# Row statistics moved to the attention stage, a split second quantiser and six unread products in the FFN stage

## The reference, cut to what matters

```
h   = h + attn(layernorm(h))
x   = layernorm(h)                                     # 192 wide
g   = gelu(quant(rmsnorm(x) * g1) @ ternary(w1).T)     # 768 wide
out = h + quant(rmsnorm(g) * g2) @ ternary(w2).T
quant(x) = round(x * 127 / max(|x|)) / (127 / max(|x|))   # per row
```

## Time and profile before

| | us |
|---|---|
| median of three runs | 1888.55 (1887.67 to 1893.47) |
| profiled execution, its own time | 1889.4 |
| its span in the trace | 1887.7 |
| attention stage with filling | about 128 to 1360 |
| FFN stage | about 1360 to 1887.7 |

### The profile page before, as it was taken

How to read it: one execution, slowest core, us unless ns; L and a number is a source line. 1 busy time by engine, 2 the same in 40 slices (tenths; PEclk the granted TensorE clock), 3 DMA queues, 4 the chain that set the end, 5 groups by cost and what they waited for, 6 DMA issues and landing times.

```text
span 1887.7 us, 50796 instructions
## 1 busy us (share of the span) xinstructions
PE 1579.8 (84%) x16574; PEld 1297.6 (69%) x16574; DVE 1364.8 (72%) x3151; ACT 1283.7 (68%) x1958; POOL 1089.7 (58%) x1503
## 2 busy tenths in 40 slices
PE   0539999999999999999999999999466666666666
PEld 0427788888888888888888888887345555555555
DVE  3636676767767676767676767676389999999996
ACT  1226666766767676767676666665288888888887
POOL 5035555555555555555555555554177777777775
PEclk9869999999999999999999999999666666666665
DMA  8674666665657565756565666660000000000000
GB/s 102 141 127 59 95 87 96 86 99 83 103 79 104 83 99 83 99 88 94 89 94 91 91 93 88 94 87 25 17 16 21 21 21 22 22 22 22 22 22 26
DMA packets 159967, 132.96 MB, mean 70 GB/s; under 512 B 32558, under 2 KB 151040, under 8 KB 159808
## 3 DMA queue, kind: packets, MB, share of 16 engines
q1 hardware_dynamic: 159168, 131.00, 44.4%
q0 software_dynamic: 768, 1.57, 0.5%
HBM read 118.32 MB, written 11.91 MB: 69 GB/s over the span
## 4 chain that ended last, share of the span: by engine, by line
PE 66%; DVE 15%; issue 7%; SPq 3%; ACT 3%; DMA 3%; POOL 1%; DVEq 1%; ACTq 0%; POOLq 0%
PE ps L1092 20%; PE ps L1176 8%; PE ps L1259 7%; PE ps L1250 7%; PE ps L1206 4%; DVE ff_st L860 4%; PE ps L1238 3%; PE ps L1232 3%; PE ps L1211 3%; PE ps L1336 2%; PE ps L1355 2%; DVE xpix L841 2%; PE ps L1167 2%; DVE xpix L853 1%; PE ps L1157 1%
## 5 line engine op out<-in xcount | busy, mean ns | idle before, releaser
L1092 PE MATMUL ps<-w_eff,pix 118*112 118x193 f32 (+1 forms) x2048 | 408.4, 337 | 25.0 <-ACT pix L909 24.3
L927 ACT ACTIVATE probs<-ps,isw 116x688 f32<-116x688 f32 x384 | 299.2, 831 | 171.6 <-PE ps L1238 171.6
L527 POOL TENSOR_TENSOR xpix<-probs,g_b 112x192 f32<-112x192 f32 (+1 forms) x512 | 296.5, 609 | 109.1 <-ACT probs L1044 99.7
L741 DVE TENSOR_REDUCE nmax<-ps 116x12 bf16<-116x1344 f32 (+2 forms) x192 | 299.6, 1560 | 80.2 <-PE ps L1211 77.7
L452 POOL TENSOR_TENSOR xsq<-xsq 118x784 f32<-118x784 f32 (+2 forms) x192 | 221.8, 1155 | 218.5 <-ACT xsq L920 208.4
L1092 PEld LDWEIGHTS ps<-w_eff,pix 118*112 118x112 f32 (+1 forms) x2048 | 309.8, 167 | 52.4 <-issue 18.9
L472 POOL TENSOR_SCALAR_AFFINE_SELECT probs<-probs 116x464 f32<-116x464 f32 x384 | 268.2, 717 | 46.5 <-ACT probs L927 31.0
L909 ACT ACTIVATE pix<-xpix 118x896 f32<-118x896 f32 (+1 forms) x128 | 198.4, 1552 | 104.9 <-DMA xpix<-in_x 56.0
L457 POOL TENSOR_TENSOR front_st<-front_st,expo 128x2 f32<-128x2 f32 x64 | 45.0, 703 | 235.2 <-DVE front_st L693 221.2
L1336 PE MATMUL ps<-w1t,xpix 96*112 96x384 f16 (+1 forms) x512 | 160.7, 488 | 14.6 <-ACT xpix L1035 13.3
L685 DVE TENSOR_SCALAR front_st<-ps 112x1 f32<-112x1 f32 (+1 forms) x128 | 18.3, 151 | 213.8 <-PE ps L1157 202.4
(11 more groups left out here) (161 smaller groups left out, 3363.3 us busy)
## 6 DMA issues: line engine op xcount, KB each, us to landing
xpix<-in_x SPq DMA_DIRECT2D x192, 196.0 KB
xpix<-in_x SPq DMA_DIRECT2D x192, 195.1 KB
rden<-den_rows SPq DMA_DIRECT2D x256, 85.5 KB, 2.1
out<-xpix SPq DMA_DIRECT2D x64, 87.0 KB
out<-xpix SPq DMA_DIRECT2D x64, 84.0 KB
xpix<-in_x SPq DMA_DIRECT2D x128, 34.1 KB
xpix<-in_x SPq DMA_DIRECT2D x128, 34.0 KB
den<-o_sb SPq DMA_DIRECT2D x256, 2.7 KB
```

What stands on the lines that cost most here:

```text
L527: last = nc.gpsimd.tensor_tensor(v2[0:P, b, tile, cols], gel[0:P, b, tile, cols], g2_b[0:P, cols], ALU.mult)
L741: V.tensor_reduce(dst, src, AX_X, ALU.max, negate=True).then_inc(s_mx, 1)
L927: A(probs[0:TB, g, 2 * e:2 * e + 2, :], ps[0:TB, 4 + 2 * e:6 + 2 * e, 0:SK], ACT.Exp, scale=isw[0:TB, 7:8]).then_inc(s_p, 1)
L1092: last = MM(ps_tok[tile][0:P, :], src, w_eff[0:HI, o, :], start=(o == 0), stop=(o == OFFS - 1))
```

## The change

1. Mean, variance, centred row and its largest magnitude are computed in the attention stage: DVE runs `measure(n - 1)` at the end of its step, POOL `row_roots(n - 2)` before `add_squares`. Means, roots and peaks of all 64 images are kept (`mean2`, `rms`, `peak`), and one short chain between the stages makes all first scales. In the FFN stage DVE only centres the row again and quantises it.
2. POOL weighs tile TB alone; DVE weighs tile TA (`weigh`). POOL also adds the epsilon and takes the root of the GELU squares (`gelu_roots`).
3. ACT quantises only tile TA of the second product; DVE quantises TB (`quantise_second`). Both now follow one step later than before (image i-2 in step i).
4. PE's order: the first product directly behind its transposes, then `turn_second(i - 2)`, `ffn_second(i - 3)`.
5. Behind `ffn_second` PE makes six products of 384 columns into bank 0 that nobody reads (`keep_busy`).

```diff
+            def row_roots(m):
+                pool.wait_ge(s_var2, m + 1)
+                nc.gpsimd.tensor_tensor(rms[:, bass.ds(m * 2, 2)], ln_st[:, 32:34], expo[:, 0:2],
+                                        ALU.pow).then_inc(s_rms, 1)
...
+            def weight(n, b):
+                after(pool, f_q2[1], n - 1)
+                pool.wait_ge(f_g, 2 * n + 2)
+                for lo in range(0, HIDDEN, HIDDEN // 4):
+                    cols = slice(lo, lo + HIDDEN // 4)
+                    last = nc.gpsimd.tensor_tensor(v2[0:TB, b, 1, cols], gel[0:TB, b, 1, cols],
+                                                   g2_b[0:TB, cols], ALU.mult)
+                last.then_inc(f_v2[1], 1)
+
+            def gelu_roots(n, b):
+                pool.wait_ge(f_ssq, 2 * n + 2)
+                apart(pool)
+                nc.gpsimd.tensor_scalar(ff_st[:, b, 18:20], gel_sum[:, b, :], EPS_RMS, None,
+                                        ALU.add).then_inc(f_var, 1)
+                pool.wait_ge(f_var, n + 1)
+                nc.gpsimd.tensor_tensor(ff_st[:, b, 20:22], ff_st[:, b, 18:20], expo[:, 0:2],
+                                        ALU.pow).then_inc(f_r1, 1)
...
+            def measure(n):
...
+                dve.wait_ge(s_h2, n + 1)
+                apart(dve)
+                for tile, P in enumerate((TA, TB)):
+                    last = V.bn_stats(ln_st[0:P, 20 + 6 * tile:26 + 6 * tile], h_all[0:P, hcols(n, tile)])
+                chain(last, 1)
+                apart(dve)
+                for tile, P in enumerate((TA, TB)):
+                    last = V.bn_aggr(ln_st[0:P, 34 + 2 * tile:36 + 2 * tile], ln_st[0:P, 20 + 6 * tile:26 + 6 * tile])
+                chain(last, 2)
+                after(dve, s_rms, n)
+                V.tensor_scalar(ln_st[:, 32:34], ln_st[:, 35:38:2], 1.0 + EPS_RMS,
+                                EPS_LN * EPS_RMS, ALU.mult, ALU.add).then_inc(s_var2, 1)
+                V.tensor_copy(mean2[:, bass.ds(n * 2, 2)], ln_st[:, 34:38:2])
+                for tile, P in enumerate((TA, TB)):
+                    last = V.scalar_tensor_tensor(v1[0:P, tile, :], h_all[0:P, hcols(n, tile)],
+                                                  ln_st[0:P, 34 + 2 * tile:35 + 2 * tile], g1_b[0:P, :],
+                                                  ALU.subtract, ALU.mult)
+                chain(last, 3)
+                for tile, P in enumerate((TA, TB)):
+                    last = V.tensor_reduce(peak[0:P, bass.ds(n * 2 + tile, 1)], v1[0:P, tile, :], AX_X, ALU.max,
+                                           apply_absolute_value=True)
+                last.then_inc(s_peak, 1)
...
+            def quantise_first(n):
+                dve.wait_ge(f_v1, n + 1)
+                after(dve, f_t1, n)
...
+            def final(n, b):
+                dve.wait_ge(f_m2, n + 1)
+                after(dve, f_out, 32 * n)
...
+            def second_scales(n, b):
+                st = ff_st[:, b, :]
+                after(dve, f_q2[0], n - 1)
+                dve.wait_ge(f_r1, n + 1)
+                flink(V.tensor_tensor(st[:, 28:30], st[:, 20:22], st[:, 26:28], ALU.mult))
+                flink(V.tensor_scalar(st[:, 28:30], st[:, 28:30], 1e-5, None, ALU.max))
+                flink(V.reciprocal(st[:, 32:34], st[:, 28:30]))
+                assert flinks[0] == F_LINKS
+                V.tensor_scalar(st[:, 42:44], st[:, 28:30], isw[:, 5:6], None, ALU.mult)
+                V.scalar_tensor_tensor(st[:, 38:40], st[:, 32:34], 127.0, st[:, 20:22],
+                                       ALU.mult, ALU.mult).then_inc(f_sc, 1)
...
+            def ffn_step(i, b, new=True, late=True, mid=True, last_=True):
+
                 if new:
...
+                    centre(i + 1)
+                    quantise_first(i + 1)
                 if mid:
...
+                    weigh(i - 1, 1 - b)
+                if late:
+                    quantise_second(i - 2, b)
+                if mid:
+                    peaks(i - 1, 1 - b)
                 if last_:
...
+                    final(i - 3, 1 - b)
                 if mid:
...
+                    second_scales(i - 1, 1 - b)
...
+            def keep_busy(count):
+
+                for k in range(count):
+                    MM(ps[:, 0, 0:HIDDEN // 2], w1t[0:HALF, 0, 0:128], w1t[0:HALF, 1, 0:HIDDEN // 2],
+                       start=True, stop=True)
+
+            def ffn_step(i, new=True, late=True, last_=True):
                 if new:
                     turn_first(i + 1)
+                    ffn_first(i + 1)
+                if late:
+                    turn_second(i - 2)
                 if last_:
-                    ffn_second(i - 2)
-                if new:
-                    ffn_first(i + 1)
-                if mid:
-                    turn_second(i - 1)
+                    ffn_second(i - 3)
+                if new and late:
+                    keep_busy(6)
```

More of the change, by code:

```diff
@@ L509, in _ @@
             step_images(IMAGES - 1, 0, None, newer=False, newest=False)
[L511 to L537, removed]
+            row_roots(IMAGES - 2)
+            row_roots(IMAGES - 1)
+            def weight(n, b):
[6 more added lines that the diff above has]
+                last.then_inc(f_v2[1], 1)
@@ L538, in _ @@
+            gelu_roots(0, 0)
+            weight(1, 1)
+            gelu_roots(1, 1)
+            with pool.Fori(1, PAIRS) as t:
                 for b in range(2):
[L539 to L542, removed]
+                    weight(2 * t + b, b)
+                    gelu_roots(2 * t + b, b)
         @block.vector
@@ L569, in _ @@
             step(V.memset(nmax[:, :, :], 0.0))
+            for filled in (mean2, rms, peak):
+                step(V.memset(filled[:, :], 1.0))
             dve.wait_ge(s_const, 32)
@@ new lines, in centre @@
+            def centre(n):
+                after(dve, f_q1, n)
+                for tile, P in enumerate((TA, TB)):
+                    ins = V.scalar_tensor_tensor(v1[0:P, tile, :], h_all[0:P, hcols(n, tile)],
+                                                 mean2[0:P, bass.ds(n * 2 + tile, 1)], g1_b[0:P, :],
+                                                 ALU.subtract, ALU.mult)
+                ins.then_inc(f_v1, 1)
+            def quantise_first(n):
+                dve.wait_ge(f_v1, n + 1)
+                after(dve, f_t1, n)
+                for tile, P in enumerate((TA, TB)):
+                    ins = V.tensor_scalar(q1[0:P, tile, :], v1[0:P, tile, :], scale1[0:P, bass.ds(n * 2 + tile, 1)],
+                                          MAGIC16, ALU.mult, ALU.add)
+                ins.then_inc(f_q1, 1)
@@ new lines, in quantise, with copy_first @@
+            def quantise(n, b):
+                act.wait_ge(f_sc, n + 1)
+                after(act, f_t2, n)
+                A(q2[0:TA, 0, :], v2[0:TA, b, 0, :], ACT.Copy, bias=MAGIC16,
+                  scale=ff_st[0:TA, b, 38:39]).then_inc(f_q2[0], 1)
+            def copy_first(m):
+                act.wait_ge(f_t1, m + 1)
+                after(act, f_m1, 2 * m)
+                for tile, P in enumerate((TA, TB)):
+                    src = bank16(0, 4 * TB, F16).rearrange("p (t c k) -> p t c k", t=2, c=2)
+                    ins = A(q1T[0:HALF, tile, :, 0:P], src[0:HALF, tile, :, 0:P], ACT.Copy, bias=-MAGIC16)
+                ins.then_inc(f_t1s, 1)
@@ new lines, in copy_second, with gelus @@
+            def copy_second(j):
+                act.wait_ge(f_t2, j + 1)
+                after(act, f_m2, j)
+                for tile, P in enumerate((TA, TB)):
+                    src = bank16(6 + tile, NCH * TB, F16).rearrange("p (c k) -> p c k", c=NCH)
+                    ins = A(q2T[:, tile, :, 0:P], src[:, :, 0:P], ACT.Copy, bias=-MAGIC16)
+                ins.then_inc(f_t2s, 1)
+            def gelus(m, b):
+                for tile in range(2):
+                    after(act, f_v2[tile], m - 1)
+                for tile, P in enumerate((TA, TB)):
+                    act.wait_ge(f_m1, 2 * m + tile + 1)
+                    A(gel[0:P, b, tile, :].rearrange("p (c d) -> p c d", c=2),
+                      ps[0:P, 2 + 2 * tile:4 + 2 * tile, 0:HIDDEN // 2], ACT.Gelu,
+                      scale=step1[0:P, bass.ds(m * 2 + tile, 1)]).then_inc(f_g, 1)
@@ new lines, in gelu_squares, with ffn_step @@
+            def gelu_squares(m, b):
+                after(act, f_r1, m - 1)
+                for tile, P in enumerate((TA, TB)):
+                    act.wait_ge(f_g, 2 * m + tile + 1)
+                    A(gsq[0:P, tile, :], gel[0:P, b, tile, :], ACT.Square, scale=HIDDEN ** -0.5,
+                      accum_out=gel_sum[0:P, b, tile:tile + 1]).then_inc(f_ssq, 1)
+            def ffn_step(i, b, new=True, late=True):
+                if new:
+                    copy_first(i + 1)
+                if late:
+                    quantise(i - 2, b)
+                if new:
+                    gelus(i + 1, 1 - b)
+                if late:
+                    copy_second(i - 2)
```

(5 more changed lines are left out.)

205 lines of the change are left out of this document (81 added, 124 removed).

## The result

The changed kernel takes 2032.28 us in the median (1999.21 to 2130.68, 4 runs) against 1890.22 us before: 7.5% more by the medians. The recorded ratio is 1.0654, 95% interval 1.0517 to 1.0791, because it leaves out as slow the executions that are over 1.5% above the shortest, and so counts two of six, 1999.21 and 2028.88 us. The forecast was 2012 us, 6.5% slower, with a range of 1925 to 2050. Four of the six executions took 2028.88 to 2034.27 us, so some 2030 us is this kernel's usual time, and the first experiment finds it again. The profiled execution took 1999.21 us, span 1997.5, and is the only one of that length.

What follows compares the result with a forecast made beforehand. Before, PE bounds the attention stage and mostly DVE the FFN stage; after, a closed loop sets the FFN step, T = 10.1 us. Span 1415 + 59T = 2011, median 2012 us, 6.5% slower, range 1925 to 2050.

Steps and rivals of the forecast that it cites:

- The attention stage: DVE's added measure, about 2.65 us, fits into its 2.85 us wait; cost taken as nothing, kept at 0 to 25 us.
- The closed loop: FFN stage: each step runs q1, transposes, copy, first product, transposes, second product, final, scales, centre, q1; 7.5 to 10.5 us.
- Rival 5: FFN stage: the loop is not closed, some part runs ahead; T about 7.2, 1841 us; shares rival 1's 8%.
- rival 4: POOL stretches DVE's part, some 0.8 us, or the attention stage pays 25 us; 2045 to 2065 us; chance 10%.
- The wait before `final`: FFN stage: DVE waits for PE's second product before final in every step, 2 to 4 us.
- The size of the loop: FFN stage, one trip: 10.53 us at the lower clock level, 7.47 us at the higher.
- rival 1: FFN stage: the clock stays high, T = 7.47, 1857 us; chance 8%, and 3% that it ends within 0.3%.
- The clock: FFN stage: clock at 0.5 when the first product runs, step 10.1 us; a mean above 0.85 would refute it.
- rival 2: FFN stage: first product at the higher clock level every other step; T = 8.2 to 9.4, 1935 us; chance 17%.
- The six unread products: FFN stage, behind ffn_second on PE: 1.93 us at the lower level, beside DVE's 3.03 us, so they delay nothing.
- The ends: FFN stage: q1 of image 4 at 1382, 33 us from last q1 to end; together off by up to 6 us.
- 1415 + 59T: Forecast span in us: 1382 + 33 for the ends plus 59 closed FFN steps of T = 10.1 each, giving 2011.

Runs made afterwards that it cites:

- the first experiment: The changed kernel repeated with no edit: 2032.87 us in the median, ratio 1.0748 to the kernel before.
- pe_back: Changed kernel with PE's second product put back behind the first transposes, all else kept: 1811.04 us, ratio 0.9582 to the kernel before.
- q1_ahead: Changed kernel with DVE's centre and q1 of image i+2 put ahead of final(i-3): 1838.49 us, ratio 0.9715 to the kernel before.
- peaks_late: Changed kernel with DVE's peaks of GELU moved from ahead of final(i-3) to behind it: 2141.58 us, ratio 1.1281 to the kernel before.
- fill0: Changed kernel with the six unread products taken out: 2033.54 us, ratio 1.0737 to the kernel before.

## Why the prediction was right, point by point

**The attention stage paid almost nothing: right.** The parts that the prediction lists for `measure` add up to 2.71 us, not 2.65. DVE's work per step grew by 96 / 800 x 18.7 = 2.2 us, and its wait before the patch statistics shrank from 2.85 us to 0.34:

```profile
718.18 0.61 DVE L802 TENSOR_REDUCE peak<-tok_t 112x192 f32 x2
719.13 0.16 DVE L702 TENSOR_SCALAR front_st<-ps 112x1 f32<-112x1 f32 x1 [0.34 <-PE ps L1229]
```

The last round of `maxima` repeats every 18.71 us after and 18.70 before (52 distances each). The final addition of the stage came 2.9 us later, 1362.42 after 1359.53; of this 0.7 us is there at image 0's last maximum (151.24 against 150.53), before the steady steps; where the rest arises was not traced.

**The closed loop: right, and shown three ways.** It opens on PE (pe_back), it opens on DVE (q1_ahead), and it grows by what is put into it (peaks_late). Rival 5, a loop that is not closed, is out. So is the first half of rival 4: from 1420 to 1760 us `q1` took 0.32 us a tile on average, as in its pairs of 0.55 and not of 0.95. The wait before `final` is there in every step, 3.5 us on average where the forecast said 2 to 4.

**The size of the loop: right at the lower level, too short at the higher.** The sum at the lower level was 10.53 us; the trip above took 10.64 with a block at the lower level but for its end. The terms came out as 0.61, 0.60, 5.56, 0.65 and 3.22 for 0.61, 0.60, 5.85, 0.44 and 3.03. The clock rose before the second product ended, which the 5.85 left out, and the hop from PE to DVE is 0.33 instead of 0.11. At the higher level the sum was 7.47. The step from 1724.93 to 1732.89 ran its products there and took 7.96:

```profile
1725.54 0.40 PE L1397 MATMUL ps<-ident_h,xpix 112*96 112x112 f16 x4 [2.30 <-DVE xpix L883]
1726.80 1.50 PE L1408 MATMUL ps<-w1t,xpix 96*112 96x384 f16 x8 [0.85 <-ACT xpix L1092]
1728.13 0.77 PE L1419 MATMUL ps<-ident_h,probs 112*128 112x112 f16 x12
1728.74 1.16 PE L1427 MATMUL ps<-w2t,xpix 128*112 128x192 f16 x12
```

PE's block took 3.10 (1726.80 to 1729.90) for 3.00, DVE's part and the hops 3.86 for 3.47. Even a clock that stayed high (rival 1) would so have given 7.96 us, where the forecast let the change pay below 8.01, and with the ends as measured (12 us longer, below) it pays below 7.81: no gain.

**The clock: right in kind.** It was 0.77 over the stage of the profiled run and 0.69 in the repeated one, where rival 1 needed above 0.85. The mean step of 9.67 us in the one and 10.25 in the other lie on both sides of the forecast 10.1. "At 0.5 when the first product runs" holds for most steps only: of the six that repeat in the profiled run, the first product took 2.81 us in three, 2.46 in one, and 1.50 and 1.53, the higher level, in two; in the repeated run 2.80 in five and 1.50 in one. What rival 2 described, the first product at the higher level in every other step, was thus there in part. In the trip shown above the clock comes back late in the block and falls in the pause behind it (third number from the end):

```profile
1709.90:1710.80 0.90, 0.90 (x9) 0.90 (x8) 0.00 (x0) 0.15 (x1) 0.00 (x0) 0.50 0.00 0
1710.80:1711.70 0.90, 0.90 (x10) 0.90 (x9) 0.00 (x0) 0.00 (x0) 0.00 (x0) 0.71 0.00 0
1713.50:1714.40 0.90, 0.00 (x0) 0.00 (x0) 0.65 (x4) 0.90 (x3) 0.00 (x0) 1.00 0.36 102
1714.40:1715.30 0.90, 0.00 (x0) 0.00 (x0) 0.77 (x4) 0.49 (x2) 0.00 (x0) 0.68 0.27 86
```

It rises in the second product, stays high through the six unread products and DVE's part, where PE has nothing to gain from it, and falls before the next transposes. PE's pause had begun at 1712.75 and was 1.7 to 2.5 us old. By the Trainium skill (TensorE: Matmul & The Clock Gate, "Why this matters for your kernels") a pause as short as this would not lower the clock; the trace does not agree. Nor does such a pause alone bring it down: in `q1_ahead` PE pauses for the copy 2.5 us in every step (124.7 us in 49), and the clock is 0.99. In the changed kernel it also falls while PE works, at 1735.2 in a first product. What makes it fall or rise is open. Whether transposes count as work for the clock, no run here shows.

**The six unread products: right that they are hidden, and their worth depends on the ring.** They end 2.7 us before PE's next work. With the ring closed, fill0 shows no difference. With it open they seem to help: the step is 6.47 us with them and 6.81 without in the profiled executions, but the ratios (0.9582 and 0.9647) leave it unsettled. In the kernel before they are worth 0.6%.

**The ends: the term that was mis-sized.** The forecast had a span of 1415 + 59T. With the measured mean step it gives 1986 us for the profiled run (1997.5 measured) and 2020 for the repeated one (2031.1), 12 and 11 us short, where 6 were allowed. The last `q1` to the end took 32.4 us (forecast 33), but `q1` of image 4 ended at 1387.95 instead of 1382. Most of that was there at image 0, whose `q1` ended at 1369.36 where the forecast took over the 1364.57 of before; the attention stage had ended 2.9 us later. And the first closed step, from image 4 to image 5, took 16.15 us, not one of 10. PE is behind at that point, since its first products waited for ACT's copies while the ring was open:

```profile
1388.66 2.81 PE L1408 MATMUL ps<-w1t,xpix 96*112 96x384 f16 x8 [2.74 <-ACT xpix L1092]
...
1394.11 0.37 PE L1397 MATMUL ps<-ident_h,xpix 112*96 112x112 f16 x4
...
1396.20 1.79 PE L1408 MATMUL ps<-w1t,xpix 96*112 96x384 f16 x8 [1.72 <-ACT xpix L1092]
...
1401.06 0.74 DVE L891 SCALAR_TENSOR_TENSOR xpix<-ps,ff_st,h_all 112x192 f32<-112x192 f32 x2 [5.99 <-PE ps L1427]
```

When `q1` of image 4 is done, PE still has the first product of image 3 to make. It takes up image 4 at 1394.11, 6.2 us after that `q1`, and the first `final` waits for the end of that block. The long first step is in all kernels that keep the ring (16.15 to 17.78 us), and it is 9.88 to 11.47 in those that open it.

Against the median of 2032 us the forecast is 20 us short, 9 by T (10.1 for 10.25) and 11 by the ends. Against the profiled 1999 us it is 13 us long, 25 too much by T and 12 too little by the ends. That its 6.5% meets the recorded 6.5% is in part luck: that ratio is made of one execution near either time, and the repeated kernel loses 7.5%.

The sign and the mechanism were right for the right reason, then: the decisive step was the added wait of `final`. What the other parts of the change gain together was there too, 4.2% by pe_back, and hidden behind that wait.

## What to carry to other kernels

When a reorder puts a producer into the same step as its consumer, follow the chain once around: if what stands behind the consumer on its engine feeds the producer's next start, the step is the sum of the ring, whatever the engines' busy shares say. Such a ring shows itself in a profile as two engines that wait for each other once in every step while all of them have idle time; it can be opened at either end, and here moving twelve products was worth 11%, and moving the centring and the first quantisation 10%. Work added to hold PE's clock up can pay only where someone waits for PE's products while they run at the higher clock: six unread products brought nothing in the closed ring, 0.6% in the kernel before, and about as much, unsettled, in the open one.

## What the runs showed of the hardware

The same kernel has two steady patterns in its FFN stage, each repeating over six steps with the lengths of PE's products: mean steps of 9.67 and 10.25 us, 1999 and 2033 us in all. A difference of 1.7% between two executions was here no noise but two patterns, so a kernel whose clock changes within its loop should be timed several times and its steps looked at one by one.

In the trip shown, VectorE quantises 116 x 768 numbers from single to half precision in 0.61 us (L926) and multiplies 112 x 768 in 0.95 (L900); ScalarE's quantisation of 112 x 768 takes 0.93 (L1084).
